# Attention scores from two fp32r parts on half the array rows each, in place of three bf16 parts on 98 rows

## The reference, cut to what matters

```python
q = _apply_rope(q, cos, sin)
k = _apply_rope(k, cos, sin)
scores = jnp.einsum('bhsd,bhed->bhse', q, k) * scale
attn = jax.nn.softmax(scores, axis=-1)
out = jnp.einsum('bhse,bhed->bhsd', attn, v)
...
x = x + _L0_attn_ref(_layernorm(x, axis=-1), ...)
x = x + _L0_ffn_ref(_layernorm(x, axis=-1), ...)
```

## Time and profile before

| | us |
|---|---|
| median of 3 runs | 1200.81 (1198.04 to 1201.31) |
| profiled execution, its own time | 1205.98 |
| its span, first to last instruction | 1204.1 |
| TensorE busy (matmul) | 974.9 (81%) |
| VectorE busy | 828.1 (69%) |
| ScalarE busy | 697.5 (58%) |
| GpSimd busy | 424.8 (35%) |
| granted TensorE clock, mean | 0.906 of full |

### The profile page before, as it was taken

How to read it: one execution, slowest core, us unless ns; L and a number is a source line. 1 busy time by engine, 2 the same in 40 slices (tenths; PEclk the granted TensorE clock), 3 DMA queues, 4 the chain that set the end, 5 groups by cost and what they waited for, 6 DMA issues and landing times.

```text
span 1204.1 us, 18696 instructions
## 1 busy us (share of the span) xinstructions
PE 974.9 (81%) x5241; PEld 414.1 (34%) x5313; DVE 828.1 (69%) x1622; ACT 697.5 (58%) x905; POOL 424.8 (35%) x360
## 2 busy tenths in 40 slices
PE   4608897889679897987778997888799999996564
PEld 1302222233233443333233343323343344344243
DVE  5732102669658797677676799586867897797797
ACT  2318895856448574765448665675567676771232
POOL 2413303433244333533235333542232333233243
PEclk9858998989889999988799898999989899997587
DMA  4254454324424252434413345352534353421011
GB/s 150 74 108 79 102 104 99 88 74 97 116 59 130 77 117 82 102 96 95 119 37 103 98 108 118 71 128 67 114 86 107 97 125 82 101 76 58 31 53 31
DMA packets 80001, 110.08 MB, mean 91 GB/s; under 512 B 22523, under 2 KB 56707, under 8 KB 76803
## 3 DMA queue, kind: packets, MB, share of 16 engines
q1 hardware_dynamic: 61444, 83.47, 29.9%
q10 hardware_dynamic: 18432, 25.17, 7.0%
HBM read 82.89 MB, written 25.69 MB: 90 GB/s over the span
## 4 chain that ended last, share of the span: by engine, by line
PE 49%; DVE 25%; issue 13%; ACT 4%; DMA 3%; POOL 2%; SPq 2%; another core or an unknown queue 1%; DVEq 0%; ACTq 0%; POOLq 0%
PE OP L687 13%; PE S L673 12%; PE D L659 8%; DVE th_sb L1103 3%; DVE act_sb L1108 3%; PE A L642 3%; PE D L569 3%; PE D L586 3%; PE BB L642 3%; DVE acc L1098 2%; DVE g_sb L1086 2%; DVE l_sb L1088 2%; DMA X<-in_x 2%; DVE xn L946 2%; ACT probs L804 2%
## 5 line engine op out<-in xcount | busy, mean ns | idle before, releaser
L804 ACT ACTIVATE probs<-S 128x1024 f32<-128x1024 f32 x512 | 511.8, 1022 | 256.2 <-PE S L673 253.4
L673 PE MATMUL S<-Qs,Ks 98*128 98x512 bf16 x1024 | 312.4, 399 | 61.8 <-issue 23.0
L687 PE MATMUL OP<-probs,V 128*17 128x512 f32 x2048 | 280.1, 620 | 2.7 <-ACT O L813 2.7
L891 POOL TENSOR_TENSOR act_lo<-act_sb,act_hi 128x512 fp32r<-128x512 f32 x128 | 165.5, 1293 | 212.3 <-DVE act_hi L1114 152.4
L673 PEld LDWEIGHTS S<-Qs,Ks 98*128 98x128 bf16 x1024 | 81.4, 101 | 249.0 <-ACT probs L804 98.7
L659 PE MATMUL D<-W,act_hi 128*128 128x256 f32 x448 | 135.6, 333 | 29.5 <-DVE Vn L986 16.2
L1098 DVE SCALAR_TENSOR_TENSOR acc<-D,combh,acc 128x256 f32<-128x256 f32 x224 | 97.1, 475 | 82.5 <-PE D L659 82.1
L1103 DVE SCALAR_TENSOR_TENSOR th_sb<-th_sb,g_sb 128x512 f32<-128x512 f32 x128 | 129.6, 1012 | 0.7 <-ACT th_sb L780 0.7
L885 POOL TENSOR_SCALAR W<-W2b 128x512 fp32r<-128x512 bf16 x64 | 45.4, 709 | 217.4 <-PE D L659 212.1
L1108 DVE SCALAR_TENSOR_TENSOR act_sb<-l_sb,th_sb 128x512 f32<-128x512 f32 x128 | 107.2, 837 | 16.7 <-POOL act_lo L891 12.2
L659 PE MATMUL D<-W,act_lo 128*128 128x256 f32 x448 | 116.3, 290 | 0.0
(11 more groups left out here) (136 smaller groups left out, 1016.7 us busy)
## 6 DMA issues: line engine op xcount, KB each, us to landing
W<-in_w ACTq DMA_DIRECT2D x64, 256.0 KB, 2.7
Ks<-k_scr SPq DMA_DIRECT2D x32, 384.0 KB
W2b<-in_w ACTq DMA_DIRECT2D x64, 128.0 KB, 2.7
Ks<-k_scr SPq DMA_DIRECT2D x32, 256.0 KB
o_scr<-O SPq DMA_DIRECT2D x32, 256.0 KB, 4.5
q_scr<-parts SPq DMA_DIRECT2D x16, 384.0 KB, 3.1
k_scr<-parts SPq DMA_DIRECT2D x16, 384.0 KB, 2.6
Qs<-q_scr SPq DMA_DIRECT2D x32, 192.0 KB
```

The lines of the kernel that those rows point to most:

```text
L673: last = mm(S[:, j2, C * i:C * (i + 1)], Ks[0:SROWS + MROWS, g % 2, j, P * kt:P * (kt + 1)], Qs[0:SROWS + MROWS, g % 2, j, :], start=True, ...
L687: last = mm(OP[32 * j:32 * j + VW, :], V[:, kt, HG * g + j, :], probs[:, s % 2, C * j:C * (j + 1)], start=kt == 0, stop=kt == KT - 1)
L804: nc.scalar.activation(probs[:, s % 2, 2 * C * j2:2 * C * (j2 + 1)], S[:, j2, :], ACT.Exp, scale=SCALE).then_inc(exp_done, 1)
L891: tt(act_lo[:, e % 2, it, :], act_sb[:, a % 2, :], act_hi[:, e % 2, it, :].bitcast(FP32), ALU.subtract).then_inc(lo_s, 1)
```

## The change

q and k are split into two fp32r parts (high and low) in place of three bf16 parts. The three products high x high, high x low and low x high take 48 rows, and one row more is the shift, 49 in all. Two heads stand at a time: heads 0 and 1 of a group on rows 0 to 48, heads 2 and 3 on rows 64 to 112. A pair of score products is now one head of each half, and `block_of` finds a head's block in probs. The array is used for scores as two tiles of 64 rows by 128 columns.

- Removed: ScalarE's second rounding (L761), DVE's third part (L966), the DMA of ones into Ks.
- Changed: GpSimd's subtraction (L865 before) writes the low part at once, in stage `part2`; rounding writes fp32r; the scratch of q, k and the shift is fp32 with 2 parts, so a tile writes 512 KB where it wrote 384 KB. Qs and Ks have the same bytes per partition (2 heads of 4 bytes for 4 of 2).
- Added: `stack` issues 8 DMAs of parts and 2 of the shift in place of 6 and 1; the bytes into Qs and Ks are the same (96 rows, 4 KB and 8 KB each). DVE fills rows 32 to 63 and 96 to 127 of Ks with ones (two MEMSETs of 32x4096) in the stage `weights` of the head.
- The number of score products, their 512 columns, and their place in TensorE's order are as before.

```diff
-SROWS = 6 * HD
-MROWS = 2
+PAIRED = 2 * HD
+HALF = P // 2
+SROWS = 3 * HD
...
-PRODUCTS = ((0, 3), (1, 2), (2, 1))
...
-        parts = sb("parts", [P, 2, 3, C], BF16)
+        parts = sb("parts", [P, 2, 2, C], FP32R)
...
-        Qs = sb("Qs", [P, 2, HG, C], BF16)
-        Ks = sb("Ks", [P, 2, HG, L], BF16)
+        Qs = sb("Qs", [P, 2, HG // 2, C], FP32R)
+        Ks = sb("Ks", [P, 2, HG // 2, L], FP32R)
...
+        def rows_of(j, shifts):
+            return slice(HALF * (j // 2), HALF * (j // 2) + SROWS + shifts)
+        def block_of(j):
+            return 2 * (j % 2) + j // 2
...
-                    sp.dma_start(Qs[rows, g % 2, :, :].rearrange("p j t -> p (j t)"),
...
-                    sp.dma_start(Ks[rows, g % 2, :, :].rearrange("p j t -> p (j t)"),
-                                 k_scr[b, 0:blocks, ch, :].rearrange("a (d j) t -> d a (j t)", j=HG)).then_inc(signal, 16)
...
+                for h in range(2):
+                    high = slice(HALF * h, HALF * h + PAIRED)
+                    low = slice(HALF * h + PAIRED, HALF * h + SROWS)
...
+                    sp.dma_start(qs[high, :], q_of[h, 0][:, None, :].to_broadcast([HD, 2, HG // 2 * C])).then_inc(signal, 16)
+                    sp.dma_start(ks[high, :], k_of[h].rearrange("a d t -> d a t")).then_inc(signal, 16)
+                    sp.dma_start(qs[low, :], q_of[h, 1]).then_inc(signal, 16)
+                    sp.dma_start(ks[low, :], k_of[h, 0]).then_inc(signal, 16)
...
                 for i in range(2):
-                    j = 2 * j2 + i
-                    last = mm(S[:, j2, C * i:C * (i + 1)], Ks[0:SROWS + MROWS, g % 2, j, P * kt:P * (kt + 1)],
-                              Qs[0:SROWS + MROWS, g % 2, j, :], start=True, stop=True)
+                    rows = rows_of(2 * i + j2, True)
+                    last = mm(S[:, j2, C * i:C * (i + 1)], Ks[rows, g % 2, j2, P * kt:P * (kt + 1)],
+                              Qs[rows, g % 2, j2, :], start=True, stop=True)
...
-                elif st == "part2":
-                    act.wait_ge(qk_r1, 4 * u + a + 1)
-                    nc.scalar.copy(parts[:, a % 2, 1, :], sw[:, a % 2, :]).then_inc(qk_p2, 1)
...
-                elif st == "length":
+                elif st == "part2":
                     pool.wait_ge(qk_p1, 4 * u + a + 1)
-                    tt(sw[:, a % 2, :], rot[:, a % 2, :], parts[:, a % 2, 0, :], ALU.subtract).then_inc(qk_r1, 1)
+                    tt(parts[:, a % 2, 1, :], rot[:, a % 2, :], parts[:, a % 2, 0, :].bitcast(FP32), ALU.subtract).then_inc(qk_p2, 1)
...
-                    v.memset(Mt[:, :, :], 0.0).then_inc(c_set2, 1)
+                    v.memset(Mt[:, :].bitcast(FP32), 0.0).then_inc(c_set2, 1)
+                    for h in range(2):
+                        v.memset(Ks[HALF * h + PAIRED:HALF * (h + 1), :, :, :].bitcast(FP32), 1.0).then_inc(c_set2, 1)
...
-                elif st == "part3":
-                    dve.wait_ge(qk_p2, 4 * u + a + 1)
-                    v.tensor_tensor(parts[:, a % 2, 2, :], sw[:, a % 2, :], parts[:, a % 2, 1, :], ALU.subtract).then_inc(qk_p3, 1)
```

More of the change, by code:

```diff
@@ L70, in block_kernel @@
         place(PREP, h, ("qk", a))
-        for st in ("rope", "part1", "length", "part2", "part3"):
+        for st in ("rope", "part1", "length", "part2"):
             place(PREP, h + AT[st], (st, a))
@@ L85, in block_kernel @@
     for f in range(NF + LAG):
-        h = FFN0 + (f * 3 // 2 * 2 if PAIRED else 3 * f)
+        h = FFN0 + f * 3 // 2 * 2
         if f >= LAG:
@@ L91, in block_kernel @@
     for f in range(NF):
-        h, after = (FFN0 + (i * 3 // 2 * 2 if PAIRED else 3 * i) for i in (f, f + 1))
+        h, after = (FFN0 + i * 3 // 2 * 2 for i in (f, f + 1))
         for st, off in (("tanh", TANH), ("hidden", HIDDEN), ("w2", W2AT), ("lo", LO)):
             place(EXPERTS, (after + off - 2) if off >= 2 else h + off, (st, f))
-    h = FFN0 + ((NF + LAG - 1) * 3 // 2 * 2 if PAIRED else 3 * (NF + LAG - 1)) + 1
+    h = FFN0 + (NF + LAG - 1) * 3 // 2 * 2 + 1
     FINAL = h // 2
@@ L110, in block_kernel @@
         if i >= 2:
-            HEAD += [("length", *tile[2]), ("part2", *tile[2]), ("part3", *tile[2])]
+            HEAD += [("length", *tile[2]), ("part2", *tile[2])]
         if i < 4 * NCH:
@@ L188, in scratch @@
             return nc.dram_tensor(name, shape, dt, kind="Internal").ap()
-        q_scr = scratch("q_scr", (B, NCH, 3, E, C), BF16)
-        k_scr = scratch("k_scr", (B, 3, E, L), BF16)
-        m_scr = scratch("m_scr", (B, MROWS, H, L), BF16)
+        q_scr = scratch("q_scr", (B, NCH, 2, E, C), FP32)
+        k_scr = scratch("k_scr", (B, 2, E, L), FP32)
+        m_scr = scratch("m_scr", (B, H, L), FP32)
         o_scr = scratch("o_scr", (B * NCH, NG, P, C), FP32)
@@ L433, in stage @@
                     for i in range(B):
-                        sp.dma_start(m_scr[i].rearrange("r h t -> h r t"), Mt[:, :, :]).then_inc(m_zero, 16)
+                        sp.dma_start(m_scr[i], Mt[:, :].bitcast(FP32)).then_inc(m_zero, 16)
                 elif st == "x_in":
@@ L438, in stage @@
                     sp.dma_start(X[:, :, :], x_v[bass.ds(u, 1)].rearrange("o p t c -> (o p) t c")).then_inc(x_ld, 16)
-                elif st == "part3":
-                    sp.wait_ge(qk_p3, 4 * u + a + 1)
+                elif st == "part2":
+                    sp.wait_ge(qk_p2, 4 * u + a + 1)
                     ch = slice(P * (a % 2), P * (a % 2 + 1))
                     to = q_scr[bb, n, :, ch, :] if a < 2 else k_scr[bb, :, ch, C * n:C * (n + 1)]
-                    sp.dma_start(to.rearrange("a p t -> p a t"), parts[:, a % 2, :, :]).then_inc(scr_w[a % 2], 16)
+                    sp.dma_start(to.rearrange("a p t -> p a t"), parts[:, a % 2, :, :].bitcast(FP32)).then_inc(scr_w[a % 2], 16)
                 elif st == "x1_in":
@@ L718, in turn @@
                                     for hf in range(2):
-                                        last = mm(S[:, i % 2, C * hf:C * (hf + 1)], Qs[0:SROWS, g % 2, j, P * t:P * (t + 1)],
-                                                  Ks[0:SROWS, g % 2, j, C * hf:C * (hf + 1)], start=True, stop=True)
+                                        last = mm(S[:, i % 2, C * hf:C * (hf + 1)], Qs[rows_of(j, False), g % 2, j % 2, P * t:P * (t + 1)],
+                                                  Ks[rows_of(j, False), g % 2, j % 2, C * hf:C * (hf + 1)], start=True, stop=True)
                                     last.then_inc(ex_mm, 1)
```

56 lines of the change are left out of this document (25 added, 31 removed), and 2 rows, old and new, of the table AT.

## The result

| | median of the runs (range) |
|---|---|
| before | 1201.06 us of 4 (1198.04 to 1205.74) |
| after | 1237.48 us of 4 (1235.72 to 1249.39) |
| ratio | 1.0321, interval 1.0248 to 1.0394 |

The account below looks back on a forecast made before the run. TensorE was taken as the main bound (49% of the chain), with ScalarE also near its limit in chunk 0. Scores -17.1, parts -4.6, head +1.8 and queue +4 sum to -15.9 us from 1200.81: 1185 us, range 1145 to 1240.

Parts of the forecast that it names:

- Parts, -4.6: In the chunks, 24 tiles lose 0.67 us on DVE and 0.62 on ScalarE, weighted by chain share: -4.6 us.
- SyncE's queue: Three more DMAs per stack: 1 us before the first scores and 1 at each of three X loads, +4 us.
- rival 2: Scores: the two halves' loads go one after the other; +28 us, 1213 us, slower; chance 0.17.
- rival 5: Chunks: TensorE's granted clock falls, more stretches at 1.2 GHz; about +30 us on the path, 1215 us; chance 0.07.
- Scores, -17.1 us: All chunks: overlapping pairs save TensorE 14.1 us per chunk, less shape changes and exposed loads; weighted by chain, -17.1 us.
- rival 1: Scores: changing between 64 and 128 rows is free and the first load hides; 1127 us; chance 0.12.
- rival 3: Scores: the array's halves do not overlap, a pair stays at 0.44 us; 1260 us, slower; chance 0.12.
- Rival 4: The path moves off TensorE; X, DVE's experts and GpSimd fill the gaps in chunks 0 to 5; 1200 us; chance 0.12.
- head, +1.8: Before attention: third part's removal gives -4.6 and -0.6 us, two fills of Ks cost +7.0; sum +1.8 us.

Follow-up runs that it names:

- e1: Changed kernel with SyncE's write of a tile's parts put back from 5 to 10 half-steps after the projection; 1208.31 us, 1.0038 of the kernel before.
- e4: Kernel before with SyncE's write of a tile's parts moved from 10 to 7 half-steps after the projection; 1219.97 us, 1.0164 of the kernel before.
- e3: e1 with scores over all 128 rows in one array shape, Qs's unfilled rows zeroed (output differs); 1207.4 us, 1.0048 of the kernel before.
- e9: e1 with only the first 512 of each exponential's 1024 columns computed; 1201.24 us, 0.9999 of the kernel before.
- e10: e3 with only the first 512 of each exponential's 1024 columns computed; 1207.32 us, 1.0047 of the kernel before.
- e2: e1 with the two fills of Ks moved on DVE to right behind the first copy of the normed X; 1200.03 us, 0.9989 of the kernel before.
- e11: Kernel before with the load of X issued ahead of the stack at the end of each batch's first chunk; 1190.52 us, 0.9913 of the kernel before.

## Why the prediction was wrong

**The step that failed.** The prediction put the move of SyncE's write at nothing. Its part on the parts says that the larger writes "go while the queue has many steps of time; they hide behind attention", and its part on SyncE's queue says of the output's way that it "waits behind the stack too; GpSimd and the output projection are next in line, and I count nothing", and that "within a chunk a stack is due a whole group later, and a late issue hides". It never priced the move of the write from 10 half-steps to 5, which the diff does by dropping `part3`. It is worth 29.2 us (the changed kernel against e1), and 17.5 when the old kernel does it (e4). The stack is indeed due late; what is hurt is the output's write behind it, through it DVE's reciprocal, and through that TensorE, which waits and then runs at the lower clock. Without this term the forecast would have been compared with 1208, still a miss by 23. The measured 1237 lies inside the stated 1145 to 1240 by luck: the upper end was there for rivals 2 and 5, and none of the five names the write.

**Scores, -17.1 us.** This term is the second miss. Measured about nothing: e1 is 0.9 slower than e3 and 6 slower than the kernel before; e9 is 6 faster than e10. In chunk 7, at full clock and with TensorE as the bound, 3.1 us were forecast (3.4 at 0.9), and e1 took 0.2 more than before. The pairs' overlap was right (0.22 plus the change, 0.43 measured for 0.41), and rivals 1, 2 and 3 fell with it: the shape costs, both loads go in 0.19, and the halves overlap. I did not have the exposed first load of D, nor ScalarE. The first makes a step with work in place 0 lose 0.12 to 0.16 where the sum had between a gain of 0.06 and a loss of 0.05, and chunks 1 to 7 have 20 to 25 such steps each. For the second, the prediction saw that chunk 0 has TensorE and ScalarE "near their limit" and still weighed TensorE's microsecond with 0.5 there; its plain steps gained 0.11 of 0.36. Halving the exponentials moves the comparison of tiles and full rows by 7 us (0.9 behind to 6 ahead), so ScalarE does not carry the whole miss. Rival 4, that the path moves off TensorE, gave 1200 us and is near e1 and e2 in time; but chunk 7 shows that already TensorE's own saving failed to come, and no run separates the rest. That two tiles may load and stream in parallel is also what the Trainium skill says (TensorEngine Tiling (Array Packing), Key Properties), and the row at 454.33, two loads in 0.19, agrees. Its other rule there, that a change of mode drains the engine, agrees as well: D's load starts at 454.75, 0.01 before its product, where loads within one shape start 0.12 ahead.

**The clock, rival 5 (0.07).** It is partly right, in two places. The larger one is group 1 of chunks 0 to 5 of the changed kernel, where TensorE's busy time grew by 15 us; there the clock fell behind a wait that the write had made, not for shorter streaming. The other is the scores' own. The first group of chunk 0, before and then e1, in the view of stretches:

```profile
88.60:116.40 27.80, 25.12 (x120) 6.42 (x121) 6.20 (x19) 21.35 (x25) 9.63 (x8) 0.90 0.40 74
```

```profile
91.00:122.40 31.40, 27.09 (x121) 8.63 (x121) 6.21 (x19) 21.34 (x25) 9.65 (x8) 0.79 0.38 70
```

0.90 against 0.79 of full, so more of the stretch at 1.2 GHz, with TensorE busy for 90% of the one and 86% of the other. These two are far apart for their kinds: the same group had 0.75 to 0.87 in the traces with tiled scores, 0.85 to 0.90 in those with the old ones, and 0.92 and 0.87 in e3 and e10. The mean clock over all runs of e1 is 0.897 (0.865 to 0.907), of the kernel before beside it 0.911, and of e3 0.923 (0.920 to 0.928): e1's and e3's ranges do not meet. A straight line through the 21 runs of before has 5.3 us for 0.01 of clock, with much scatter (a correlation of 0.55); from that, e3's 0.026 above e1 would be an estimated 14 us, near the 17 forecast for the tiles. Chunk 7, where all three ran at full clock and the tiles kept their 2.0 us, fits that: eight such chunks would be an estimated 16. That the clock takes back the rest is argued, since no run holds the clock fixed.

**Parts, -4.6, and head, +1.8.** Head measured +2.2 (attention from 88.6 to 90.8), with the fills at 8.3 for 7.0 (e2 against e1) and the removal at about 6.2 for 5.2. The parts' term cannot be separated from the scores'. e2 against before is -2.4 in all.

**SyncE's queue, +4.** The ten DMAs took 7.1 us for 6.4. The forecast priced 1 us at each of three chunk starts for the three DMAs more ahead of X. No run measures that by itself: e11 moves X ahead of the whole stack, in the kernel before, and gives 11 us, of which 5 are in chunk 1's first group.

## What to carry to other kernels

When a change removes a stage, look at every DMA that goes with it: moved up in an in-order queue, a write that isn't ready blocks transfers that have nothing to do with it (29 us here, with the same instructions on TensorE). Ask of each waiting DMA what stands behind it, and who waits for that, before pricing the arithmetic. And before pricing faster matmuls, read the floor of the engine that consumes them in the steps where the saving is due.

## What was not expected of the hardware

- Two fp32r products of 49 rows on the two halves of the array run and load side by side: 0.22 us of streaming and one load record of 0.19 us for the pair.
- A change between tiles of 64 rows and of 128 rows costs 0.09 to 0.11 us each way plus the exposed first load of the next run, as the values' change does.
- Behind a wait of 3.67 us for DVE, TensorE's granted clock was 0.50 for the next 9.3 us, and 8 products of values took 1.91 us where they take 1.05. In the same groups of e1, without that wait, it was 1.00.
- Kernels with shorter pairs of scores were granted a lower clock in all their runs (e1 0.897, e9 0.900, against e3 0.923 and e10 0.921), though they were no slower.
